# Graph kernel on one core: a maximum split into groups, one more early block, two more early groups, and direct gathers begun in emptied ring places

## The reference

```python
# layer 0: a gated message per edge, summed at its source node
z = jnp.concatenate([x[src], x[dst], edge_feats], axis=1) @ W.T + b
z = (z - mean(z)) * rsqrt(var(z) + BN_EPS) * gamma + beta
msg = sigmoid(z[:, :H]) * softplus(z[:, H:])
x = layernorm(x + x + zeros.at[src].add(msg))
# layer 1: mean of the neighbours, a small MLP, a gain by their distance
local_mean = segment_sum(x[src], dst) / maximum(cnt, 1)
feature_diff = tanh(norm(x - local_mean))
h = x + ALPHA * (relu(x @ W1 + b1) @ W2 + b2) * feature_diff
x = layernorm(x + (h - mu) * rsqrt(var + LN_EPS) * gamma + beta)
```

## Time and profile before

| what | us |
|---|---|
| time before, median of 3 runs | 3820.1 (3819.95 to 3830.05) |
| profiled execution, own time | 3820.0 |
| its span | 3818.3 |
| message stage, first maximum to last add | 2304 to 2926 |
| averaging stage, first direct gather to last add | 2979 to 3743 |

### The profile page before, as it was taken

One profiled execution on the slowest core, in us unless ns is written; L12 is line 12 of the kernel. 1 busy time (PEld: TensorE's weight loads), 2 busy tenths in 40 slices (PEclk: granted clock), 3 DMA queues, 4 the chain that ended last, 5 costly groups with the idle time before them and its releaser, 6 DMA issues. The chain is left out here.

```text
span 3818.3 us, 83823 instructions
## 1 busy us (share of the span) xinstructions
PE 3044.3 (80%) x18854; PEld 2156.6 (56%) x18855; DVE 2763.0 (72%) x7466; ACT 2218.7 (58%) x6111; POOL 2573.1 (67%) x2634
## 2 busy tenths in 40 slices
PE   6875999999988999999999976767776577767661
PEld 2322333333336777777777765656665466666661
DVE  6567888888875555555555548999998688888787
ACT  1423999999984666666666659989996010000003
POOL 2667777777776777777777760028887677777770
PEclk8986999999999999999999997888987789888885
DMA  7433333333336888888888884557774433333321
GB/s 201 129 109 100 108 101 108 102 106 107 101 95 200 264 263 264 264 263 263 263 263 264 260 296 172 200 196 275 275 270 133 112 81 77 80 80 80 75 69 41
DMA packets 315282, 640.18 MB, mean 168 GB/s; under 512 B 54446, under 2 KB 188759, under 8 KB 306999
## 3 DMA queue, kind: packets, MB, share of 16 engines
q0 software_dynamic: 99584, 247.90, 22.8%
q1 hardware_dynamic: 173416, 267.88, 22.4%
q10 hardware_dynamic: 42192, 123.38, 8.8%
HBM read 425.59 MB, written 213.37 MB: 167 GB/s over the span
## 5 line engine op out<-in xcount | busy, mean ns | idle before, releaser
L372 POOL DMA_INDIRECT rec_d<-arena x830 | 798.9, 963 | 345.0 <-issue 335.0
L871 POOL DMA_INDIRECT arena<-b_tab,arena x880 | 832.3, 946 | 281.1 <-issue 262.3
L783 PE MATMUL psum<-arena 128*128 128x440 f16 x3360 | 720.5, 352 | 50.5 <-ACT arena L466 50.0
L892 DVE TENSOR_TENSOR arena<-psum,arena 128x512 f32<-128x512 f32 x440 | 283.5, 686 | 544.1 <-DMA arena<-b_tab,arena 303.5
L634 DVE TENSOR_SCALAR arena<-iota_t,arena 128x880 f16<-128x880 f16 x840 | 523.8, 666 | 109.6 <-PE psum L783 102.6
L982 PE MATMUL psum<-weT,arena 128*128 128x256 f32 x1760 | 545.1, 392 | 45.3 <-DVE arena L892 41.9
L466 ACT ACTIVATE arena<-arena 128x128 f16<-128x128 f16 x1680 | 561.7, 386 | 0.0
L783 PEld LDWEIGHTS psum<-arena 128*128 128x128 f16 x3360 | 288.2, 97 | 477.1 <-issue 160.6
L1596 PE MATMUL psum<-arena,x_sb 128*128 128x129 f32 x2368 | 329.4, 304 | 158.8 <-DVE x_sb L1483 105.7
L1475 DVE TENSOR_TENSOR arena<-psum,arena 128x258 f32 x880 | 374.7, 426 | 83.6 <-PE psum L1596 77.5
L985 PE MATMUL psum<-arena 128*128 x2640 | 432.5, 273 | 0.0
(11 more groups left out here) (265 smaller groups left out, 5574.7 us busy)
## 6 DMA issues: line engine op xcount, KB each, us to landing
z_d<-arena ACTq DMA_DIRECT2D x220, 512.0 KB
arena<-z_d SPq DMA_DIRECT2D x44, 2560.0 KB
arena<-rec_d SPq DMA_DIRECT2D x220, 260.0 KB
arena<-in_edge_attr SPq DMA_DIRECT2D x83, 640.0 KB, 4.8
arena<-early_d SPq DMA_DIRECT2D x36, 516.0 KB
arena<-b_tab,arena POOLq DMA_INDIRECT x880
rec_d<-arena POOLq DMA_INDIRECT x831, 2.1
early_d<-arena POOLq DMA_DIRECT2D x9, 1032.0 KB, 5.2
```

The lines of the kernel that those rows point to most:

```text
L372: nc.gpsimd.indirect_dma_start(rec_rows, bass.IndirectOffsetOnAxis(e_idx[:, s, k:k + 1], 0), e_buf[:, s, k, :], None).then_inc(s_es[s], 16)
L783: last = nc.tensor.matmul(bank(4 + 2 * k + h)[:, 0:HALF], hot_lane[:, s, k, :], hot_tile[:, s, h * HALF:(h + 1) * HALF], start=start, stop ...
L871: nc.gpsimd.indirect_dma_start(bg[:, s, k, :], None, b_tab, bass.IndirectOffsetOnAxis(rec[:, s, k, H:H + 1].bitcast(I32), 0)).then_inc(s_b ...
```

## The change

`EARLY` goes from 36 to 38 and `EARLY_BLOCKS` from 16 to 17; `EARLY_TILES` stays at 300. The averaging stage then has 38 early and 72 direct groups: two early groups first, then the 18 rounds, and no direct groups left over. The waits that count products are shifted by the two leading groups.

VectorE's step takes the maximum group by group: maximum, add of the previous chunk's group, product, one-hots. `s_spl` counts groups, and ScalarE's waits on it are for five times as many. The register loads of `adds` now stand ahead of the first maximum.

Direct gathers use the ring place that follows the last early group (`ring_place`). GpSimd waits for the store of the last group but one ahead of the first direct gather, stores the last two early groups ahead of the second direct group, and waits for that store ahead of the third.

```diff
-EARLY, EARLY_BLOCKS, EARLY_TILES = 36, 16, 300
+EARLY, EARLY_BLOCKS, EARLY_TILES = 38, 17, 300
...
-        ROUNDS = EARLY // 2
+        ROUNDS = DIRECT // 4
+        AHEAD_EARLY = EARLY - 2 * ROUNDS
...
+        def ring_place(s):
+            return (s + EARLY) % XS
...
+            for n in range(AHEAD_EARLY):
+                step(n, n, "early", n, n % 2, n // 2 + 1, before)
+                before = (n, n, "early", n)
             for i in range(HEAD):
                 round_of(i)
             with eng.Fori(HEAD, ROUNDS) as it:
                 round_of(it)
-            for j, n in enumerate(range(4 * ROUNDS, DIRECT)):
-                step(6 * ROUNDS + j, j, "direct", n, n % XS, n // XS + 1, before)
...
-                keep(EARLY // 2 - 1)
-                for i in range(2):
-                    pool.wait_ge(s_be[i], len(range(i, EARLY // 2, 2)) * 16)
...
+                def stored(q):
+                    pool.wait_ge(s_be[q % 2], (q // 2 + 1) * 16)
...
                 def gather(n, s, use):
+                    if isinstance(n, int):
+                        if n == 0:
+                            stored(LAST - 1)
+                        if n == 1:
+                            keep(LAST)
+                        if n == 2:
+                            stored(LAST)
                     wait(pool, s_gi, n + 1)
...
-                        wait(act, s_spl, c + (i - 1))
+                        wait(act, s_spl, CG * c + (CG * i - CG))
...
-                    nc.vector.scalar_tensor_tensor(v, ex[:, j % 2, :, :], -1.0, v, ALU.mult, ALU.max).then_inc(s_spl, 1)
                     dve.wait_ge(s_sig, c + 1)
                     before = not (isinstance(c, int) and c == 0)
                     if before:
                         firsts = adds(c - 1)
-                    dve.wait_ge(s_spl, c + 1)
                     for g in range(CG):
-                        nc.vector.tensor_tensor(u[:, g, :], u[:, g, :], v[:, g, :], ALU.mult).then_inc(s_msgT, 1)
+                        nc.vector.scalar_tensor_tensor(v[:, g, :], ex[:, j % 2, g, :], -1.0, v[:, g, :], ALU.mult, ALU.max).then_inc(s_spl, 1)
                         if before:
                             add(c - 1, (j - 1) % CS, g, firsts[g])
+                        dve.wait_ge(s_spl, CG * c + (g + 1))
+                        nc.vector.tensor_tensor(u[:, g, :], u[:, g, :], v[:, g, :], ALU.mult).then_inc(s_msgT, 1)
                         hots(c, g)
```

More of the change, by code:

```diff
@@ L1179, in build @@
         DIRECT = N_GROUPS - EARLY
-        ROUNDS = EARLY // 2
+        ROUNDS = DIRECT // 4
+        AHEAD_EARLY = EARLY - 2 * ROUNDS
         RING = 6
-        assert 4 * HEAD >= 2 * len(CH) + 1 and EARLY % 2 == 0 and DIRECT >= 4 * ROUNDS and 6 * G % RING == 0
+        assert 4 * HEAD >= 2 * len(CH) + 1 and AHEAD_EARLY >= 0 and AHEAD_EARLY % 2 == 0 and DIRECT == 4 * ROUNDS and 6 * G % RING == 0
         def first_tile(kind, n):
             return n * G if kind == "early" else n * G + EARLY * G
+        def ring_place(s):
+            return (s + EARLY) % XS
         def turns(eng, step):
             def round_of(i):
[L1191 to L1196, removed]
+                first = AHEAD_EARLY + 6 * i
+                before = (first - 1, AHEAD_EARLY + 5, "direct", 4 * i - 1)
+                if isinstance(i, int) and i == 0:
+                    before = (first - 1, first - 1, "early", first - 1) if AHEAD_EARLY else None
+                order = (("early", 2 * i + AHEAD_EARLY, 0, i + (AHEAD_EARLY // 2 + 1)), ("direct", 4 * i, 0, i + 1), ("direct", 4 * i + 1, 1, i + 1),
+                         ("early", 2 * i + (AHEAD_EARLY + 1), 1, i + (AHEAD_EARLY // 2 + 1)), ("direct", 4 * i + 2, 2, i + 1), ("direct", 4 * i + 3, 3, i + 1))
+                for at, (kind, n, s, use) in enumerate(order):
+                    step(first + at, AHEAD_EARLY + at, kind, n, s, use, before)
+                    before = (first + at, AHEAD_EARLY + at, kind, n)
+            before = None
+            for n in range(AHEAD_EARLY):
+                step(n, n, "early", n, n % 2, n // 2 + 1, before)
+                before = (n, n, "early", n)
             for i in range(HEAD):
@@ L1201, in turns @@
                 round_of(it)
-            before = (6 * ROUNDS - 1, 5, "direct", 4 * ROUNDS - 1)
-            for j, n in enumerate(range(4 * ROUNDS, DIRECT)):
-                step(6 * ROUNDS + j, j, "direct", n, n % XS, n // XS + 1, before)
-                before = (6 * ROUNDS + j, j, "direct", n)
         with nc.Block() as block:
@@ L1243, in _ @@
                     if n >= 2:
-                        sp.wait_ge(s_sg, 24 * n - 40)
+                        sp.wait_ge(s_sg, 8 * (n - 1) if n < AHEAD_EARLY + 2 else 24 * (n - AHEAD_EARLY) - 40 + 8 * AHEAD_EARLY)
                     sp.dma_start(xb[:, n % 2, :, :].rearrange("p k f -> p (k f)"), early_d[:, n, :]).then_inc(s_xb2[n % 2], 16)
@@ L1272, in _ @@
                         keep(g // 2 - 1)
-                keep(EARLY // 2 - 1)
-                for i in range(2):
-                    pool.wait_ge(s_be[i], len(range(i, EARLY // 2, 2)) * 16)
                 def rows(s):
                     for k in range(G):
-                        nc.gpsimd.indirect_dma_start(ring_slot(s)[:, k, :], None, x1_tab, bass.IndirectOffsetOnAxis(gi[:, s, k:k + 1], 0)).then_inc(s_xe[s], 16)
+                        nc.gpsimd.indirect_dma_start(ring_slot(ring_place(s))[:, k, :], None, x1_tab,
+                                                     bass.IndirectOffsetOnAxis(gi[:, s, k:k + 1], 0)).then_inc(s_xe[ring_place(s)], 16)
                 pool.wait_ge(s_xs, 48)
                 settle(pool, s_turn)
+                LAST = EARLY // 2 - 1
+                def stored(q):
+                    pool.wait_ge(s_be[q % 2], (q // 2 + 1) * 16)
                 def gather(n, s, use):
+                    if isinstance(n, int):
[5 more added lines that the diff above has]
+                            stored(LAST)
                     wait(pool, s_gi, n + 1)
                     if s < 2:
-                        wait(pool, s_sg, 24 * (2 * use) + (8 * s - 80))
+                        wait(pool, s_sg, 24 * (2 * use) + (8 * s - 80 + 8 * AHEAD_EARLY) if not isinstance(use, int) or use > 1 else 0)
                     else:
-                        wait(pool, s_sg, 24 * (2 * use) + (8 * s - 72))
+                        wait(pool, s_sg, 24 * (2 * use) + (8 * s - 72 + 8 * AHEAD_EARLY) if not isinstance(use, int) or use > 1 else 0)
                     settle(pool, s_turn)
@@ L1293, in _ @@
                 groups(pool, gather, None, 4 * ROUNDS, XS, head=XS)
[L1294 to L1298, removed]
             @block.scalar
@@ L1514, in _ @@
                 for k in range(G):
-                    pair_add(2 * ROUNDS + DIRECT - 1, DIRECT - 1 - 4 * ROUNDS, k, pairs[k])
+                    pair_add(AHEAD_EARLY + 6 * ROUNDS - 1, AHEAD_EARLY + 5, k, pairs[k])
             @block.tensor
@@ L1590, in product @@
                     else:
-                        wait(pe, s_xe[s], use * (16 * G) + EARLY_IN[s])
-                    rows = xb[:, s, :, :] if kind == "early" else ring_slot(s)
+                        wait(pe, s_xe[ring_place(s)], use * (16 * G) + EARLY_IN[ring_place(s)])
+                    rows = xb[:, s, :, :] if kind == "early" else ring_slot(ring_place(s))
                     for k in range(G):
```

2 lines of the change are left out of this document (1 added, 1 removed).

## The result

The changed kernel takes 4106.85 us (median of 6 runs, 4102.65 to 4110.08) against 3820.8 for the kernel before (3818.34 to 3830.05): a ratio of 1.0744, with a 95% interval of 1.073 to 1.0758. It is 286 us slower, where 277 had been forecast. The profiled execution took 4104.65 us, with a span of 4102.7.

What follows compares the result with a forecast made beforehand. No single engine bounds the whole span; ScalarE waits on VectorE's maximum in the message stage, and direct gathers bound averaging. 3820.0 + 302.9 - 20.2 - 6.1 = 4096.6, so 4097 us; range 4030 to 4140.

Steps and rivals of the forecast that it cites:

- sum of the message stage: Message stage of 22 pairs, mostly 42.4 us each against 27.27: 924.8 us in total, +302.9 us.
- forecast waits of 5 and 9 us: ScalarE's second-half sigmoid in the message stage would wait twice a pair for VectorE's maximum, some 5 and 9 us.
- low clock for a and d: TensorE near 1.2 GHz from copies to first add, in both steps of a pair; full clock would give -52 us.
- 15 us more of 0.09 us an instruction: VectorE's message stage: if four extra instructions a chunk each paid 0.09 us, the result would grow by 15 us.
- Only the second sigmoid held: Message stage: first chunk's last maximum ends before ScalarE reaches it; 38.4 us a pair, 4017 us; chance 0.05.
- Not slower: Message stage unchanged, VectorE far enough ahead; early gathers run straight into direct ones; 3809 us; chance 0.04.
- part 1: VectorE's message-stage maximum taken by groups: the last maximum comes at the step's end and holds ScalarE's sigmoids, +302.9 us.
- The closed gate: Early gathers on GpSimd all come behind the stored rows, 363 us more, near 4460 us; chance 0.01.
- part 2: 17 blocks and 38 early groups: 576 direct gathers replace 592 in the averaging stage, -20.2 us.
- the end keeps its length: End of the averaging stage: the last two units are direct ones as before, so no change there.
- GpSimd the bound: Averaging stage: VectorE is busy 624.97 of 756.00 us, so at 736 us GpSimd still bounds it.
- the rival sum of 4088: Averaging stage: were the long gather only a burst of transfers, its 8.8 us could go, giving 4088; no chance given.

Runs made afterwards that it cites:

- The test of the columns: Changed kernel with ScalarE copying the first four direct groups' index columns ahead of the first relu: 4095.77 us, ratio 1.0722.
- parts 2 and 3 alone: Changed kernel with the whole-chunk maximum back at the head of VectorE's step, early groups, blocks and ring places staying changed: 3815.62 us, ratio 0.9992.

## Why the prediction was right, and where it was not

**The sum of the message stage held.** From the first maximum (2305.32 us) to the end of the last add (3230.76) it took 925.4 us; 924.8 had been forecast. The steps, as the profile after has them:

| step | forecast, us | row after, us |
|---|---|---|
| a. copies to first add | 4.1 | 2470.10 to 2474.27 = 4.2 |
| b. first add to end of last maximum | 10.4 | 2474.27 to 2484.71 = 10.4 |
| c. sigmoid to the other copies | 2.4 | 2442.13 to 2444.56 = 2.4 |
| d. the second step, from its copies (2.43 behind 2484.74) | 14.5 | its a: 2487.17 to 2491.26 = 4.1; its sigmoid 2444.56 to 2459.11 = 14.6 |
| e. second sigmoid to the next copies | 11.0 | 2459.11 to 2470.10 = 11.0 |
| pair | 42.4 | 42.61 |

The forecast waits of 5 and 9 us are the 5.96 and 9.62 of the rows. The choice of the low clock for a and d, and of a higher one in b, was right too: the granted clock was 0.50, the 1.2 GHz level, from 2470 to 2474 and from 2487 to 2491, and 0.94 between 2475 and 2483, and the transposes tell it in their durations:

```profile
2470.82 1.08 PE L1535 MATMUL psum<-ident,arena 128*128 128x128 f32 x4 [12.42 <-ACT arena L1318]
...
2475.96 0.60 PE L1535 MATMUL psum<-ident,arena 128*128 128x128 f32 x4
...
2487.89 1.09 PE L1535 MATMUL psum<-ident,arena 128*128 128x128 f32 x4 [3.86 <-ACT arena L1318]
```

**The split cost little.** Five maxima with nothing between them took 3.02 us, so the forecast's 0.15 us a chunk was 0.17, or 7.5 us over 44 chunks, and not the 15 us more of 0.09 us an instruction. The Trainium skill ("VectorE: DVE Perf Modes", "The TRN2 errata — SBUF-src ops pay a fixed extra latency per instruction") has many small tiles pay a fixed cost each; in this trace four more instructions back to back cost 0.17 us together. The totals (1.0013 with the five maxima, 0.9992 without) can't tell this cost, since most of a longer message stage is hidden there.

**The rivals.** Only the second sigmoid held (4017): both are held, 42 waits. Not slower (3809): no, but with part 1 undone its mechanism is there to be seen, at 3815.6. The limit that it set for the last maximum's end, 2.45 us behind the start of the step, was missed by 10.7 us; the prediction's 8 counted from the first add, which comes later. Its price was too low by 4.8 us at least, since an early group takes 12.5 us and it charged two at the 10.1 of a direct one. The closed gate (near 4460): the early gathers were done 235.59 us ahead, and sooner than the forecast had them (3038 against 3105), since a group took 10.6 us and not the 12.5 of the earlier trace rows.

**The averaging stage was mis-sized.** The ledger of the profiled spans, 3818.3 before and 4102.7 after:

| part of the span | change, us | forecast, us |
|---|---|---|
| ahead of the message stage | +1.2 | 0 |
| message stage | +303.5 | +302.9 |
| last add to rows stored (46.8 to 42.2) | -4.6 | 0, bound -5 |
| rows stored to first direct gather (6.0 to 0.8) | -5.2 | -6.1 |
| first direct gather to the end of the last | -14.6 | -20.2 |
| end of the last gather to the end of the span | +4.0 | 0 |

The border's store came close to its bound, which had been kept for the range and taken as nothing. Two steps failed, both in part 2. The first is that the text followed the two early units that now lead only to SP's loads, and not to what else runs in the order of the units: TensorE's first MLP product, the relu behind it, and the index column that ScalarE copies behind the relu. In the kernel before the relu began 17.8 us behind the first direct gather and cost GpSimd nothing; now it began 34.6 us behind. This took 7.05 of the 20.2 us. The second is "the end keeps its length". VectorE's 625 of 756 busy us seemed to leave room, but in the shorter stage it finished its last add 13.2 us behind the last gather's end, where it had been 7.9, and the end grew by 4.0 us. From the first direct gather to the last add, 754.4 us against 763.7 before, only 9.3 of the 20.2 us were won. The test of the columns suggests that the two failures have one root: freed of the idle, GpSimd waits 4.3 us for a product instead, and the stage wins 2.4 us. With parts 2 and 3 alone, where VectorE's adds began 20.4 us ahead of the direct gathers (18.8 behind them in the change), the last add ended 9.2 us behind the last gather. So "GpSimd the bound" seems to have been true of the kernel before, with less slack behind it than the 20 us that it was asked to carry; that VectorE's late start used this slack up is argued, not shown.

By luck, the gain that the border's store gave stood in for half of what the averaging stage withheld, so the profiled execution came out 8 us above the sum, and the median 10.

**The long gather stayed**, as the prediction had it: in every run, the gather beside VectorE's long two-input addition takes 9.2 to 9.8 us. It was the third direct gather in the earlier trace rows, the eighth here, and an early one in the test of parts 2 and 3. So none of these orders got rid of it, and the rival sum of 4088 is out. The Trainium skill ("SBUF — State Buffer", "Who interferes with whom") says that such an instruction contends with a GpSimd instruction that reads SBUF. The trace agrees, but the gather ended 3.2 us behind the addition (3292.06 and 3288.88), which the last section takes up.

## What to carry to other kernels

Before a long instruction is cut into pieces that are spread among others, ask which semaphore its end releases and how much slack that release has: here none, since ScalarE already waited 0.4 us for it, and the last piece ended 10 us later in the step, in a loop through three engines. Keep the pieces in place, or give the buffer another place first (a third one for second chunks won back 9.8 of 15.3 us a pair). A test with the same pieces put back at the head tells order from size, if it is read in the stage that it touches: the total hid most of what was left. And of work that is moved within an order shared by all engines, follow every engine's list, down to a 0.2 us copy behind a relu.

## What the runs showed of the hardware that was not expected

The long gather lasts longer than the addition that it stands beside. VectorE at that point in the kernel after:

```profile
3282.20 6.68 DVE L1522 TENSOR_TENSOR arena<-arena 128x6272 f32<-128x6272 f32 x1
3288.80 2.44 DVE L1494 TENSOR_SCALAR x_sb<-iota,l_loc 128x256 f32<-128x256 f32 x9
3292.60 0.43 DVE L1486 TENSOR_TENSOR arena<-psum,arena 128x258 f32 x1 [1.36 <-PE psum L1607]
```

The gather began at 3282.55 and ended at 3292.06, some 0.8 us behind the end (3291.24) of the nine one-hots that follow the addition without a gap. With parts 2 and 3 alone, VectorE's run of the same two instructions ended at 2987.08 and the gather at 2987.90. Whether the one-hots hold it by themselves was not tried.

It is not a pause of VectorE that lets the gather go on. In the kernel before, a gather beside a whole maximum ended soon after it, though the product followed without a gap:

```profile
2576.49 2.81 DVE L1406 SCALAR_TENSOR_TENSOR arena<-arena 128x2560 f32<-128x2560 f32 x1
2579.33 0.69 DVE L1413 TENSOR_TENSOR arena<-arena 128x512 f32<-128x512 f32 x1
```

```profile
2577.56 2.56 POOL L1269 DMA_INDIRECT arena<-x_tab,l_idx  x1 [0.30 <-issue]
```

The gather ended at 2580.12, 0.82 us behind the maximum (2579.30). In that message stage 27 early gathers took 2.4 to 3.6 us in place of 0.94, and each ended 0.80 to 0.86 us behind a maximum. So the split had a good side that was not forecast. With parts 2 and 3 alone 27 gathers beside maxima were that long; with the five maxima at the head 7 took 3.0 us or more; in the changed kernel, where the pieces lie apart, none took more than 1.30 us.
